# Ternary weight rounding moved from ScalarE to VectorE, and a row-sum transpose moved ahead of the key/value step

## The reference

```
xn = layernorm(x)                              # x: 8 x 2048 x 1024, f32
attn:  kv = xn @ Wkv                           # one key and one value head of 64
       q  = layernorm(xn, gamma) @ Wq          # 16 heads of 64
       q, k = l2norm(q) * q_scale, l2norm(k) * k_scale
       sim  = 8 * q k^T, causal, two null keys in front, the first 64 tokens see each other
       a = softmax(sim) v  ->  a @ Wout
ffn:   Wq1 = clip(round(W1 / (mean|W1| + 1e-5)), -1, 1)      # W1: 4096 x 1024
       Wq2 = clip(round(W2 / (mean|W2| + 1e-5)), -1, 1)      # W2: 1024 x 4096
       f = relu(xn @ Wq1^T + b1) @ Wq2^T + b2
y = x + a + f
```

## Time and profile before

| | us |
|---|---|
| median of 3 runs | 2006.69 |
| the profiled execution's own time | 2002.55 |
| span of its slowest core (core 6) | 2000.6 |
| spans of all cores | 1982.3 to 2000.6 |
| TensorE busy | 1511.3 (76%) |
| ScalarE busy | 613.3 (31%) |
| VectorE busy | 467.1 (23%) |
| GpSimd busy | 146.3 (7%) |

### The profile page before, as it was taken

One profiled execution on the slowest core, in us unless ns is written; L12 is line 12 of the kernel. 1 busy time (PEld: TensorE's weight loads), 2 busy tenths in 40 slices (PEclk: granted clock), 3 DMA queues, 4 the chain that ended last, 5 costly groups with the idle time before them and its releaser, 6 DMA issues.

```text
span 2000.6 us, 19968 instructions; the slowest of 8 cores (1982.3 to 2000.6 us)
## 1 busy us (share of the span) xinstructions
PE 1511.3 (76%) x5544; PEld 573.0 (29%) x5609; DVE 467.1 (23%) x1616; ACT 613.3 (31%) x1123; POOL 146.3 (7%) x217
## 2 busy tenths in 40 slices
PE   0222657766678989888999991598889898988986
PEld 0111222222222222222333330343334343433432
DVE  1334544543332333323112220100100010011000
ACT  0000322323345555556677770022002101200210
POOL 2000000000001110101111110000000000000000
PEclk9656656566587677778788996599689969977998
DMA  5122444534334443445564557311231222122123
GB/s 119 28 50 54 126 116 127 149 116 149 96 81 101 112 112 86 102 102 116 116 127 111 138 122 203 92 32 64 74 106 53 80 90 74 42 80 101 44 76 116
DMA packets 184492, 194.20 MB, mean 97 GB/s; under 512 B 114590, under 2 KB 152480, under 8 KB 183360
## 3 DMA queue, kind: packets, MB, share of 16 engines
q10 hardware_dynamic: 42336, 97.00, 15.9%
q1 hardware_dynamic: 126240, 51.40, 11.6%
q0 software_dynamic: 15808, 44.52, 8.3%
HBM read 139.26 MB, written 29.49 MB: 84 GB/s over the span
## 4 chain that ended last, share of the span: by engine, by line
PE 54%; DMA 25%; DVE 9%; issue 7%; ACT 3%; ACTq 1%; POOL 1%; DVEq 0%; SPq 0%; POOLq 0%
PE psim L1130 11%; PE psim L1154 6%; PE pav L900 6%; PE pwork L1154 5%; DMA wtout<-wqbf 5%; PE pwork L866 5%; PE psim L819 5%; PE psim L1045 3%; DMA ktok<-kvT_sb 3%; PE psim L726 3%; DMA wstage<-W 3%; DMA xnTg<-xnt 2%; DMA xbufB<-x 2%; DVE qtmp L750 2%; DMA xnT<-xnbf 2%
## 5 line engine op out<-in xcount | busy, mean ns | idle before, releaser
L832 ACT ACTIVATE attnT<-psim,negC 128x512 bf16<-128x512 f32 (+3 forms) x508 | 292.4, 622 | 188.0 <-PE psim L819 61.5
L900 PE MATMUL pav<-attnT,v_sb 128*64 128x512 bf16 (+3 forms) x640 | 275.5, 434 | 23.9 <-DVE outunT L918 22.2
L1145 ACT ACTIVATE h1full<-psim,b_sb 128x512 bf16<-128x512 f32 x128 | 86.7, 687 | 639.3 <-PE psim L1130 569.9
L1130 PE MATMUL psim<-xnTg,W1B 128*128 128x512 bf16 x1003 | 238.7, 379 | 17.6 <-ACT h1full L1145 16.5
L819 PE MATMUL psim<-qhatT,khsT 64*128 64x512 bf16 (+3 forms) x508 | 210.3, 414 | 49.6 <-ACT attnT L832 37.7
L866 PE MATMUL pwork<-attnT,dind 128*2 128x512 bf16 (+3 forms) x640 | 183.1, 450 | 0.0
L1154 PE MATMUL psim<-w2ring,h1full 128*128 128x512 bf16 x497 | 167.3, 419 | 9.3 <-DMA w2ring<-w2qt 6.8
L1154 PE MATMUL pwork<-w2ring,h1full 128*128 128x512 bf16 x503 | 170.0, 422 | 0.5
L1130 PEld LDWEIGHTS psim<-xnTg,W1B 128*128 128x128 bf16 x1024 | 99.0, 98 | 139.9 <-issue 22.8
L518 DVE TENSOR_SCALAR wqbf<-wstage 128x512 bf16<-128x512 f32 x128 | 54.7, 427 | 348.7 <-DMA wtout<-wqbf 248.5
L1045 PE MATMUL psim<-invdenT,indic 2*128 2x128 f32 x256 | 71.4, 419 | 79.0 <-DMA xnTg<-xnt 55.3
(11 more groups left out here) (142 smaller groups left out, 1184.8 us busy)
## 6 DMA issues: line engine op xcount, KB each, us to landing
wstage<-W ACTq DMA_DIRECT2D x128, 512.0 KB, 4.1
w2ring<-w2qt SPq DMA_DIRECT2D x32, 512.0 KB, 3.6
w2ring<-w2qt ACTq DMA_DIRECT2D x32, 512.0 KB, 3.3
xbufA<-x POOLq DMA_DIRECT2D x16, 512.0 KB, 4.8
w1qt<-wtout POOLq DMA_DIRECT2D x32, 256.0 KB, 3.2
w2qt<-wtout POOLq DMA_DIRECT2D x32, 256.0 KB, 3.2
xbufB<-x POOLq DMA_DIRECT2D x32, 256.0 KB, 3.6
wstage<-Wq ACTq DMA_DIRECT2D x8, 512.0 KB, 4.3
```

The lines of the kernel that those rows point to most:

```text
L832: ts_=ts_: s.activation(attnT[:, ts_, c, j0 * 128:j0 * 128 + w], ring_ap2(slot, 0, 128, 0, w), AF.Exp, bias=negC[:, 0:1]),
L900: w=w: t.matmul(pav[po:po + 64, j0 * 128:j0 * 128 + w], v_sb[:, c, :], attnT[:, ts_, c, j0 * 128:j0 * 128 + w], start=(c == 0), stop=False ...
L1130: sp=sp: tt.matmul(PM1[rot][:, 0:TW], W1B[:, c, fc * 128:(fc + 1) * 128], xnTg[:, sp, c, :], start=(c == 0), stop=(c == ND - 1)),
L1145: s.activation(h1full[:, fc, 0:TW], PM1[rot][:, 0:TW], AF.Relu, bias=b1_sb[:, fc:fc + 1]),
```

## The change

Two edits. In pass 2 the old `m_t1` multiplied by 1/scale and added a large constant that rounds to an integer, `m_t2` subtracted the constant on ScalarE, and `m_t3` clipped to -1..1. Now `m_t1` only multiplies (VectorE, L494), `m_t2` is a comparison with -0.5 on VectorE (L506), and `m_t3` compares with 0.5 and subtracts the other comparison (VectorE, L517), which takes two f32 inputs. `qsc` is now read by `m_t3` too, and `m_t1` waits for `m_t3` of both halves.

In the tiles' steps, `s_mu2t` is gone as a step of its own; its three instructions now stand first in `s_mu2xn`. A tile has 10 steps instead of 11, so the triples after the heads hold other steps, and the four tiles of a block take 14 heads instead of 15.

```diff
@@ quant_pass2c @@
-                    MAGIC, ALU.mult, ALU.add), [st["ld"], qstate["g1"],
-                                                qstate["qsc_free"][hf]])
+                    None, ALU.mult), [st["ld"], qstate["g1"],
+                                      qstate["qsc_free"]])
...
-                t2 = prog.add("scalar", lambda s, a=a, slot=slot: s.add(
+                t2 = prog.add("vector", lambda v, a=a, slot=slot:
+                              v.tensor_scalar(
                     wstage[:, slot, a:a + hw2], qsc[:, a:a + hw2],
-                    magc[:, 0:1]),
-                    [st["t1%d" % hf], t_mag])
-                qstate["qsc_free"][hf] = t2
+                    -0.5, None, ALU.is_lt), [st["t1%d" % hf]])
...
-                st["t3%d" % hf] = prog.add("vector", lambda v, a=a, slot=slot:
-                                           v.tensor_scalar(
-                    wqbf[:, 0, a:a + hw2], wstage[:, slot, a:a + hw2],
-                    1.0, -1.0,
-                    ALU.min, ALU.max), [st["t2%d" % hf], qstate["wqbf_free"]])
+                t3 = prog.add("vector", lambda v, a=a, slot=slot:
+                              v.scalar_tensor_tensor(
+                    wqbf[:, 0, a:a + hw2], qsc[:, a:a + hw2], 0.5,
+                    wstage[:, slot, a:a + hw2],
+                    ALU.is_gt, ALU.subtract),
+                    [st["t2%d" % hf], qstate["wqbf_free"]])
+                qstate["qsc_free"][hf] = t3
@@ stage0_steps @@
-        def s_mu2t():
-            nonlocal t_ptr_free
+        def s_mu2xn():
+            nonlocal t_ptr_free, xnbf_free
             t_mu2b = prog.add("vector", lambda v: v.tensor_copy(
...
-
-        def s_mu2xn():
-            nonlocal xnbf_free
             tdt = prog.dma("sync", lambda y: y.dma_start_transpose(
...
-        return [s_stats, s_ln, s_xnf, s_mu2xn, s_kv, s_kv2, s_mu2t,
-                s_qproj, s_qss, s_qinv, s_qT]
+        return [s_stats, s_ln, s_xnf, s_mu2xn, s_kv, s_kv2, s_qproj,
+                s_qss, s_qinv, s_qT]
```

More of the change, by code:

```diff
@@ L516, in go @@
                 a = hf * hw2
-                st["t3%d" % hf] = prog.add("vector", lambda v, a=a, slot=slot:
-                                           v.tensor_scalar(
-                    wqbf[:, 0, a:a + hw2], wstage[:, slot, a:a + hw2],
-                    1.0, -1.0,
-                    ALU.min, ALU.max), [st["t2%d" % hf], qstate["wqbf_free"]])
+                t3 = prog.add("vector", lambda v, a=a, slot=slot:
[5 more added lines that the diff above has]
+                qstate["qsc_free"][hf] = t3
+                st["t3%d" % hf] = t3
             return go
```

## The result

The changed kernel takes 1967.12 us (median of 10 runs) against 2003.21 us for the kernel before (10 runs). The ratio is 0.9817, 95% interval 0.9794 to 0.984: 1.8% faster, about 36 us, where 56 were forecast. The profiled execution took 1963.61 us, its slowest core (core 2) 1962.1. Comparisons leave out runs in which one die ran at a lower clock.

A forecast was written before the change was run, and what follows sets the result against it. Phase A alone could change: a start-up chain of waits, then TensorE nearly the bound in blocks 2 and 3. Gains 26 + 25 + 5 = 56 us off 2002.55 give 1946.5, as a median 1951; forecast range 1930 to 1970, wider 1905 to 1987.

The forecast's parts named there:

- The row sum, in the start-up: Start-up: casting `mu2b` at once starts query products and norms earlier, 6.4 us a tile, 26 us for four (22 to 28).
- The row sum, in the blocks: Blocks, 12 tiles: earlier queries gain 20 in block 0 plus 15 elsewhere, less 10 price: 25 us (-10 to 52).
- the discount for blocks where TensorE seemed the bound: Blocks after block 0: only half of the other 31 us of VectorE's idle time counted as gain, 15 us.
- The forecast price: Three blocks: in one tile each, TensorE waits for logarithm, exponential, normalisation and row sum; about 10 us lost.
- Pass 2: Weight rounding moved wholly to VectorE: a gain of 5 us, between -10 and +18.
- fit with 1 us to spare: Block 3 weight tile: VectorE's last four operations and handoffs take about 2.7 of the 3.8 us before the next transposes.
- falls between: Pass 2: an eviction (0.69 us) amid a tile's operations uses up the spare time; the tile costs 0 to 0.7 us more.
- ScalarE's side: Pass 2: 92.4 us of ScalarE work goes, but loads then wait for `m_t3` two tiles back; gain at most 9 + 9 us of waits.
- (a): Rival: only the start-up pays, the blocks gain nothing; 1981 us, chance 0.2.
- (b): Rival: fewer waits keep TensorE at 2.4 GHz, block 3 falls from 319 to 284 us; 1916 us, chance 0.15.
- (c): Rival: VectorE becomes the bound in pass 2, 2.0 us per weight tile in blocks 1 and 2; 2020 us, chance 0.07.
- The wait for `mu2b`: Sign, start-up and blocks: TensorE's wait for this one-column cast falls from 98.6 us to some 20.

The follow-up runs named there:

- e1_order: The changed kernel with the rounding of the kernel before put back, so only the new step order remains: 1934.58 us, ratio 0.964 to the kernel before.
- e10_dbl: The changed kernel with two buffers each for the rounded weights (`wqbf`) and their transposes (`wtout`): 1893.67 us, ratio 0.9463 to the kernel before.
- e4_three: The changed kernel with three buffers instead of two for the weights read (`wstage`): 1923.45 us, ratio 0.9574 to the kernel before.
- e3_two: The changed kernel with two VectorE operations instead of three per half weight tile, comparing the weight with plus and minus half the scale: 1949.86 us, ratio 0.9708.
- e5_store_sp: The changed kernel with the stores of the rounded weights issued on SyncE's queue instead of GpSimd's: 1957.78 us, ratio 0.9771 to the kernel before.

## Why the prediction was right, and where it was not

The direction and the range held (1951 forecast, 1905 to 1987, measured 1967). The sum of 56 us against 36 hides two errors of opposite sign.

- **The row sum, in the start-up:** forecast 26, measured 25.3 by `e1_order`. The steps came as worked out: cast at once, transpose under the wait for `xnT`, copies directly behind `khsT`.
- **The row sum, in the blocks:** forecast 25, measured 20.5 + 17.9 + 7.2 = 45.6 in blocks 0 to 2, less some 3 in block 3. I took all of block 0 and half of the others. VectorE's idle time before the copies fell by 58 of its 74.0 us (15.8 are left in `e1_order`), 22.4 of it in the start-up. Idle time of VectorE before the query copies was about the right measure, and the discount for blocks where TensorE seemed the bound was too large. The forecast price, the wait at the normalisation in one tile of a block, exists as a wait (44.6 us in all), but it cost far less than 10 us, as it mostly stands in for the wait for `xnT`: that was 15.3 + 5.7 + 11.0 = 32.0 us before in blocks 0 to 2 and is 3.4 + 1.9 + 1.2 = 6.5 after. The two waits together fell from 90.8 to 51.1.
- **Pass 2:** forecast a gain of 5, measured a loss of 30 on top of the new order (spans' blocks 1 to 3) and 31 us in the medians on its own. This step failed. For an ordinary tile the sentence that VectorE's four operations "fit with 1 us to spare" held: from a store to the next transposes it was 3.30 us in both kernels (medians of block 3, all cores), and the last `m_t3` ended 0.85 us before the transposes went out, where it had been 1.61. What broke is the price of an eviction that "falls between". I took its length, 0.69, and so 0 to 0.7 us more a tile. VectorE also waits there for TensorE's last product into `pav`. In 20 of the 248 tiles the last `m_t3` ended more than 1 us after the store before had landed. All 20 have an eviction in their midst, with a wait of 1.5 to 6.3 us, and their transposes came 13.1 us after those before; in the other tiles it was 8.4. In the kernel before there were 7 such tiles, at 9.6 us, two of them with a wait at the eviction, of 3 us. That the eviction's place is the cause is argued from these rows: no run moved it within VectorE's order. And a wait for TensorE can be a result of its lower clock as well as a cause. What `e10_dbl` shows is that block 3 is 24 us shorter with the chain overlapped, although VectorE waits more at the evictions.
- **ScalarE's side:** the load did become the new meeting point (25.3 us of waits for `wqbf`), as forecast. That its absence alone does not repair block 3 is shown by `e4_three`.
- **Rivals:** (a) did not happen. (b), the clock, went the other way: 0.88 to 0.83 in block 3; `e10_dbl` shows 0.90 when the chain is overlapped. Its price was also mis-read: the 319 us it started from reach into block 2. Block 3 itself took 264 us, less than the 284 it was to fall to. (c) had the right kind of mechanism at the wrong size: 30/64, about half a microsecond per weight tile, not 2.0, and through the chain and its effect on TensorE's waits and clock, not through VectorE's load.
- **What I named as signs:** VectorE's busy time is 583 us, not 555: 16.6 us of the difference are the scaling (128 x 0.13) and 1.7 the comparison; the lengths of the single operations do not show the other 10. The wait for `mu2b` was to fall to some 20 us and is 102.0 over the span, after 98.5. That sign was badly chosen, since a wait that changes its cause keeps its name.

How a wait of one microsecond becomes several is only partly shown. In block 3 of the changed kernel each of the nine falls of TensorE's granted clock stands beside a wait of TensorE. After those of 1.09, 1.87 and 1.83 us (at 899, 972 and 1078) the clock was at the lower level for 17 to 21 us. The length of the wait alone does not decide: after 1.55 us at 963 it was 3.4 us, and in the kernel before a wait of 0.82 us at 1054 was followed by 17 us and one of 2.31 at 1030 by 7. The Trainium skill (TensorE: Matmul & The Clock Gate, Part 1) ties the clock to TensorE's recent activity, and these rows agree. The 34 us more that block 3 spent at half the clock can account for up to 17 us, an estimate from the two profiled cores. No experiment changed a wait alone, so how much of the 30 us is clock stays open.

## What to carry to other kernels

A tiny instruction that stands behind a long chain in an in-order engine can hold another engine for as long as the chain; look for short operations with a long wait behind them and move them to where their input is ready. Before work is moved onto an engine that seems idle, ask whether that engine stands in a serial chain of single buffers: there it is the length of the stay that counts, not the busy share. And count into the stay every instruction in between that waits for another engine, at its wait and not only its length. A second buffer in the chain was worth more here than any choice of who does the rounding.

## What the runs showed of the hardware

A VectorE operation with one f32 source, from SBUF to SBUF, took longer when it began while GpSimd was issuing a store (0.89 us). In the changed kernel 393 scalings (all cores) began 0.25 to 0.32 us behind the start of a store: they took 0.76 to 0.88 us instead of 0.49. Seven that began 0.02 us behind it took their 0.49, and so did 399 comparisons of `e3_two` that began up to 0.2 us behind it (0.48). The nine operations with two f32 inputs that began during a store stayed at 0.69. With the stores on SyncE's queue no scaling took more than 0.52. The Trainium skill (SBUF — State Buffer, "Who interferes with whom") has VectorE in a two-port mode and GpSimd share one port pair under an exclusive lock, and the trace agrees.

The same 256 KB store landed in 2.6 us from SyncE's queue (`e5_store_sp`) and in 3.2 us from GpSimd's (the changed kernel), both medians over the span. From SyncE's it also went out sooner, 0.06 instead of 0.59 us after the landing of the transposes that it waited for (medians in block 3).
